# Attention heads: queries and keys in two F32R parts, scores as three passes over 64 rows

## The reference

```
q = einsum('bsd,hde->bhse', x, Wq)          # 16 heads, e = 64
k = einsum('bsd,hde->bhse', x, Wk)
v = einsum('bsd,hde->bhse', x, Wv)
scores = einsum('bhse,bhte->bhst', q, k) / sqrt(64), causal mask
out = softmax(scores) @ v
y = x + concat(out) @ Wo, then a layer norm with gamma and beta
```

## Time and profile before

| what | us |
|---|---|
| median of 3 runs | 995.03 (991.85 to 996.21) |
| the profiled execution, its own time | 994.27 |
| its span, first to last instruction | 992.5 |
| PE busy | 748.4 (75%) |
| DVE busy | 672.1 (68%) |
| ACT busy | 544.9 (55%) |
| POOL busy | 548.5 (55%) |
| PE waiting for xv_lo before value slices, 255 to 845 us | 14.9 (6 times) |
| DVE waiting for PE's masks before the maxima, 255 to 845 us | 162.8 (178 times) |
| ACT waiting for DVE's maxima, 255 to 845 us | 211.0 (180 times) |

### The profile page before, as it was taken

The page is one execution under the profiler, slowest core; times in us unless marked ns, Lnnn a source line. Parts: engine busy times, 40 slices in busy tenths (PEclk is TensorE's granted clock), DMA queues, the critical chain, the costliest instruction groups (busy, mean ns, idle before and its releaser), DMA issues.

```text
span 992.5 us, 21450 instructions
## 1 busy us (share of the span) xinstructions
PE 748.4 (75%) x7600; PEld 541.5 (55%) x7600; DVE 672.1 (68%) x1398; ACT 544.9 (55%) x1511; POOL 548.5 (55%) x552
## 2 busy tenths in 40 slices
PE   2567667427999998998999999999899996223232
PEld 2356555324576666775776766667676765122122
DVE  1579787844776776776677677677677875366755
ACT  0457566534665665665566566566566664054553
POOL 2166655621665565555555566555466665488862
PEclk9588878657999999999999999999999999555555
DMA  8111111011989999889789899798798998101101
GB/s 185 40 44 43 42 43 43 32 42 47 145 151 166 135 157 157 134 144 167 117 150 160 135 142 153 142 151 136 147 153 147 152 155 145 53 32 64 53 22 32
DMA packets 371461, 108.15 MB, mean 109 GB/s; under 512 B 348448, under 2 KB 365344, under 8 KB 371360
## 3 DMA queue, kind: packets, MB, share of 16 engines
q1 hardware_dynamic: 368096, 104.73, 58.8%
q10 hardware_dynamic: 3264, 2.10, 0.8%
HBM read 8.73 MB, written 2.10 MB: 11 GB/s over the span
## 4 chain that ended last, share of the span: by engine, by line
PE 45%; SPq 17%; POOL 11%; DVE 11%; issue 6%; DMA 5%; ACT 4%; POOLq 0%; DVEq 0%; ACTq 0%
PE wide L822 11%; SPq L998 7%; SPq L995 7%; PE bank L162 4%; PE bank L869 4%; PE bank L164 3%; PE bank L163 3%; PE wide L827 3%; PE bank L847 2%; PE bank L196 2%; POOL fn_y L355 2%; PE bank L849 2%; PE bank L848 2%; DMA prob_t<-prob_hl 2%; DVE ffn_g L422 2%
## 5 line engine op out<-in xcount | busy, mean ns | idle before, releaser
L975 POOL TENSOR_TENSOR prob_hl<-prob,prob_hl 128x768 f16<-128x768 f32 (+1 forms) x192 | 346.9, 1807 | 266.3 <-DVE prob_hl L927 266.3
L906 ACT ACTIVATE prob<-wide,neg_max 128x128 f32<-128x128 f32 (+3 forms) x512 | 264.0, 524 | 218.4 <-DVE neg_max L939 218.0
L939 DVE TENSOR_REDUCE neg_max<-wide 128x2 f32<-128x256 f32 (+3 forms) x256 | 205.4, 823 | 166.5 <-PE wide L827 166.3
L822 PE MATMUL wide<-k_sb,q_sb 64*128 64x128 f32 (+3 forms) x1024 | 193.4, 476 | 1.0 <-DVE k_sb L804 0.9
L847 PE MATMUL bank<-v_hi,prob_t 128*128 128x64 f16 x1280 | 134.9, 194 | 11.9 <-DMA prob_t<-prob_hl 11.4
L848 PE MATMUL bank<-v_lo,prob_t 128*128 128x64 f16 x1280 | 134.9, 194 | 0.0
L849 PE MATMUL bank<-v_hi,prob_t 128*128 128x64 f16 x1280 | 134.9, 194 | 0.0
L847 PEld LDWEIGHTS bank<-v_hi,prob_t 128*128 128x128 f16 x1280 | 117.5, 99 | 14.6 <-issue 12.5
L927 DVE CAST prob_hl<-prob 128x768 f16<-128x768 f32 (+1 forms) x192 | 119.6, 623 | 1.1 <-ACT prob L906 1.0
L849 PEld LDWEIGHTS bank<-v_hi,prob_t 128*128 128x128 f16 x1280 | 115.7, 99 | 0.0
L848 PEld LDWEIGHTS bank<-v_lo,prob_t 128*128 128x128 f16 x1280 | 115.6, 99 | 0.0
(11 more groups left out here) (184 smaller groups left out, 1468.4 us busy)
## 6 DMA issues: line engine op xcount, KB each, us to landing
prob_t<-prob_hl SPq DMA_TRANSPOSE x384, 3.2
x_next<-in_L_attn_a_in_features SPq DMA_DIRECT2D x8, 256.0 KB, 3.0
x_attn<-in_L_attn_a_in_features SPq DMA_DIRECT2D x8, 256.0 KB, 3.0
x_sb<-x_done SPq DMA_DIRECT2D x8, 256.0 KB, 2.3
y_res<-bn_y SPq DMA_DIRECT2D x8, 256.0 KB, 2.3
at_y<-y_res SPq DMA_DIRECT2D x8, 256.0 KB, 2.3
x_attn<-x_sb SPq DMA_DIRECT2D x8, 256.0 KB, 2.3
out_x<-x_done SPq DMA_DIRECT2D x8, 256.0 KB, 2.3
```

The source lines that it names most:

```text
L822: pe.matmul(dst[:, h, c:c + m], q[e, i * P:(i + 1) * P], k[e, 0:m], start=(i == UNIT_ROWS[u][0]), stop=False)
L906: last = act.activation(prob_2[s][:, at:at + m], score_banks(p, s)[:, h, c:c + m], ACT.Exp, bias=neg_max[p % 2][:, h, i:i + 1], accum_out= ...
L939: last = dve.tensor_reduce(neg_max[p % 2][:, :, i:i + 1], score_banks(p, s)[:, :, c:c + m], AX.X, ALU.max, negate=True)
L975: pool.tensor_tensor(prob_hl[u][:, w:2 * w], prob_2[u][:, 0:w], prob_hl[u][:, 0:w], ALU.subtract)\
```

## The change

- q_sb and k_sb are replaced by q_hi, q_lo, k_hi, k_lo (F32R, two buffers each). ACT writes q_hi from PSUM with the scale; DVE writes q_lo by a scalar_tensor_tensor, PSUM times the scale less q_hi, at the end of its s=0 work. ACT writes k_hi at s=1 behind the exponentials; DVE writes k_lo = PSUM less k_hi where it copied the keys.
- The K projection now waits for q_lo, the next Q projection and the scores for k_lo too.
- Each score matmul in fp32 becomes three in F32R, with the two heads alternating. The 128 keys of block 0 are widened to 256 (the second half is not read), so block 1 moves to column 256 of the bank.
- The copies xv_hi, xv_lo and their DMAs and wait are gone: value slices read xt_hi and xt_lo directly at the next batch's columns.
- x_beta of the back stage gets no memory of its own any more and lies in prob_2[2]. Branches for a loop variable that isn't an integer go.

```diff
-PAIR_AT = {0: 0, 1: 128, 2: 0, 3: 0}
+PAIR_AT = {0: 0, 1: 256, 2: 0, 3: 0}
...
         def values_tensor(pe, b, p):
             n = number(b, p)
-            wait(pe, "xv_in", 32 * (b + 1))
...
-            x = slice(p // 2 * P, (p // 2 + 1) * P)
+            x = slice((b + 1) * S + p // 2 * P, (b + 1) * S + (p // 2 + 1) * P)
...
-            split_product(pe, MB, xv_hi[:, x], xv_lo[:, x], wv_b_hi[:, half], wv_b_lo[:, half])\
+            split_product(pe, MB, xt_hi[:, x], xt_lo[:, x], wv_b_hi[:, half], wv_b_lo[:, half])\
...
         def project_tensor(pe, b, p, parts, done):
-            wait(pe, *(("k_sb", n) if done == "q_ps" else ("q_sb", n + 1)))
+            wait(pe, *(("k_lo", n) if done == "q_ps" else ("q_lo", n + 1)))
...
         def queries_scalar(act, b, p):
             wait(act, "q_ps", n + 1)
             wait(act, "s2", n - 1)
-            act.activation(q_sb[p % 2][:, :], QK, ACT.Copy, scale=float(E) ** -0.5).then_inc(sem("q_sb"), 1)
+            act.activation(q_hi[p % 2][:, :], QK, ACT.Copy, scale=float(E) ** -0.5).then_inc(sem("q_hi"), 1)
+
+        def queries_vector(dve, b, p):
+            n = number(b, p)
+            wait(dve, "q_hi", n + 1)
+            dve.scalar_tensor_tensor(out=q_lo[p % 2][:, :], in0=QK, scalar=float(E) ** -0.5,
+                                     in1=q_hi[p % 2][:, :].bitcast(F32), op0=ALU.mult, op1=ALU.subtract)\
+                .then_inc(sem("q_lo"), 1)
+
+        def keys_scalar(act, b, p):
+            n = number(b, p)
+            wait(act, "k_ps", n + 1)
+            wait(act, "s2", n - 1)
+            act.copy(k_hi[p % 2][:, :], QK).then_inc(sem("k_hi"), 1)
 
         def keys_vector(dve, b, p):
             n = number(b, p)
-            wait(dve, "k_ps", n + 1)
-            wait(dve, "s2", n - 1)
-            dve.tensor_copy(k_sb[p % 2][:, :], QK).then_inc(sem("k_sb"), 1)
+            wait(dve, "k_hi", n + 1)
+            dve.tensor_tensor(k_lo[p % 2][:, :], QK, k_hi[p % 2][:, :].bitcast(F32), ALU.subtract)\
+                .then_inc(sem("k_lo"), 1)
 
         def pair_scores(pe, b, p, u):
...
             for i in UNIT_ROWS[u]:
-                c, m = PAIR_AT[i], (i + 1) * P
-                for h in range(2):
-                    e = slice(h * E, (h + 1) * E)
-                    pe.matmul(dst[:, h, c:c + m], q[e, i * P:(i + 1) * P], k[e, 0:m], start=(i == UNIT_ROWS[u][0]),
-                              stop=False)
+                c, m = PAIR_AT[i], max(2, i + 1) * P
+                rows = slice(i * P, (i + 1) * P)
+                for a, (q, k) in enumerate(((qh, kh), (qh, kl), (ql, kh))):
+                    for h in range(2):
+                        e = slice(h * E, (h + 1) * E)
+                        pe.matmul(dst[:, h, c:c + m], q[e, rows], k[e, 0:m],
+                                  start=(i == UNIT_ROWS[u][0] and a == 0), stop=False)
...
         def heads_scalar(act, b, p):
                 if s == 0 and pair_exists(*later(b, p)):
                     queries_scalar(act, *later(b, p))
+                if s == 1 and pair_exists(*later(b, p)):
+                    keys_scalar(act, *later(b, p))
                 if s == 1 and pair_exists(*earlier(b, p, 2)):
                     wait(act, "ctx_t_ps", n - 1)
                     wait(act, "y_ps", n - 2)
                     act.copy(ctx_t[:, :], MB[:, :]).then_inc(sem("ctx_t"), 1)
...
         def heads_vector(dve, b, p):
                         values_vector(dve, bv + 1, pv, MB)
+                    if pair_exists(*later(b, p)):
+                        queries_vector(dve, *later(b, p))
                 if s == 1 and pair_exists(*later(b, p)):
                     keys_vector(dve, *later(b, p))
...
         def heads_sync(sp, b, p):
-            if p == 0 and (not isinstance(b, int) or b < B - 1):
-                wait(sp, "v_ps", VSLICES * (b + 1))
-                wait(sp, "bn_xt_lo", B)
-                for dst, src in ((xv_hi, xt_hi), (xv_lo, xt_lo)):
-                    sp.dma_start(dst[:, :].bitcast(F32), src[:, bass.ds((b + 1) * S, S)].bitcast(F32))\
-                        .then_inc(sem("xv_in"), 16)
...
-        x_beta = sb("x_beta", [P, QB, P])
+        x_beta = prob_2[2][:, 0:512].rearrange("p (a d) -> p a d", d=P)
```

More of the change, by code:

```diff
@@ L153, in hybrid_kernel @@
         prob_t = [sb(f"prob_t{u}", [P, 16, P], F16) for u in range(NU)]
[L154 to L157, removed]
+        q_hi = [sb(f"q_hi{k}", [P, S], F32R) for k in range(2)]
+        q_lo = [sb(f"q_lo{k}", [P, S], F32R) for k in range(2)]
+        k_hi = [sb(f"k_hi{k}", [P, S], F32R) for k in range(2)]
+        k_lo = [sb(f"k_lo{k}", [P, S], F32R) for k in range(2)]
         ctx_sb = sb("ctx_sb", [P, QB, 2, E])
@@ L728, in pair_exists @@
         def pair_exists(b, p):
-            return not isinstance(b, int) or 0 <= HP * b + p < PAIRS
+            return 0 <= HP * b + p < PAIRS
         def earlier(b, p, n):
@@ L767, in values_tensor @@
             n = number(b, p)
-            wait(pe, "xv_in", 32 * (b + 1))
-            if isinstance(b, int) and n < 2:
+            if n < 2:
                 wait(pe, "v_lo", n + VSLICES)
             wait(pe, "ctx_t", n - 1)
-            x = slice(p // 2 * P, (p // 2 + 1) * P)
+            x = slice((b + 1) * S + p // 2 * P, (b + 1) * S + (p // 2 + 1) * P)
             half = slice(p % 2 * 512, (p % 2 + 1) * 512)
-            split_product(pe, MB, xv_hi[:, x], xv_lo[:, x], wv_b_hi[:, half], wv_b_lo[:, half])\
+            split_product(pe, MB, xt_hi[:, x], xt_lo[:, x], wv_b_hi[:, half], wv_b_lo[:, half])\
                 .then_inc(sem("v_ps"), 1)
@@ L809, in pair_scores @@
             if u == 0:
-                wait(pe, "q_sb", n + 1)
-                wait(pe, "k_sb", n + 1)
+                wait(pe, "q_lo", n + 1)
+                wait(pe, "k_lo", n + 1)
             if u == 2:
@@ L816, in pair_scores @@
             dst = score_banks(p, u)
-            q, k = q_sb[p % 2], k_sb[p % 2]
+            qh, ql, kh, kl = q_hi[p % 2], q_lo[p % 2], k_hi[p % 2], k_lo[p % 2]
             for i in UNIT_ROWS[u]:
-                c, m = PAIR_AT[i], (i + 1) * P
-                for h in range(2):
-                    e = slice(h * E, (h + 1) * E)
-                    pe.matmul(dst[:, h, c:c + m], q[e, i * P:(i + 1) * P], k[e, 0:m], start=(i == UNIT_ROWS[u][0]),
-                              stop=False)
+                c, m = PAIR_AT[i], max(2, i + 1) * P
[5 more added lines that the diff above has]
+                                  start=(i == UNIT_ROWS[u][0] and a == 0), stop=False)
             for i in UNIT_ROWS[u]:
@@ L855, in context_turn_tensor @@
             wait(pe, "ctx", n + 1)
[L856 to L859, removed]
+            wait(pe, "v_lo", min(n + 2 + VSLICES, PAIRS))
             transposes(pe, MB, ctx_sb[:, :, :, :].rearrange("p a h e -> p (a h e)"), QB).then_inc(sem("ctx_t_ps"), 1)
@@ L890, in heads_tensor @@
                         context_turn_tensor(pe, *earlier(b, p, 2))
-                if s == 2 and (not isinstance(b, int) or b < B - 1):
+                if s == 2 and b < B - 1:
                     values_tensor(pe, b, p)
@@ L957, in heads_vector @@
                     bv, pv = before
-                    if not isinstance(bv, int) or 0 <= bv < B - 1:
+                    if 0 <= bv < B - 1:
                         values_vector(dve, bv + 1, pv, MB)
+                    if pair_exists(*later(b, p)):
+                        queries_vector(dve, *later(b, p))
                 if s == 1 and pair_exists(*later(b, p)):
                     keys_vector(dve, *later(b, p))
-                if s == 1 and p == 2 and (not isinstance(b, int) or b > 0):
+                if s == 1 and p == 2 and b > 0:
                     wait(dve, "y_ps", n - 2)
@@ L979, in heads_sync @@
             n = number(b, p)
-            if p == 0 and (not isinstance(b, int) or b < B - 1):
-                wait(sp, "v_ps", VSLICES * (b + 1))
-                wait(sp, "bn_xt_lo", B)
-                for dst, src in ((xv_hi, xt_hi), (xv_lo, xt_lo)):
-                    sp.dma_start(dst[:, :].bitcast(F32), src[:, bass.ds((b + 1) * S, S)].bitcast(F32))\
-                        .then_inc(sem("xv_in"), 16)
             if pair_exists(b, p):
-                if not isinstance(b, int):
-                    sp.to_reg(n)
-                    sp.to_reg(n + 1)
                 for u in range(NU):
@@ L1166, in _ @@
             queries_scalar(act, 0, 0)
+            keys_scalar(act, 0, 0)
             over_pairs(act, heads_scalar)
@@ L1177, in _ @@
                 values_vector(dve, 0, k, VB[k % len(VB)])
+            queries_vector(dve, 0, 0)
             keys_vector(dve, 0, 0)
```

## The result

The kernel after takes 1002.13 us (median of 4 runs, 1001.76 to 1003.28) against 994.68 us for the kernel before beside it: a ratio of 1.008, 95% interval 1.0056 to 1.0105. It is slower by 7 to 8 us. The forecast was 998, with slower as the likeliest of the three signs.

The account below looks back on a forecast made before the run. PE bound the old kernel at 8.93 us a pair; VectorE-ScalarE handovers would bind the new at 9.3. 56 x 9.3 + 7 x 8.9 + 4.2 = 587.3 against 585.3, plus 1.4 start-up: +3.4, 998 us, range 982 to 1014.

Parts of the forecast that it names:

- the three signs: Whole kernel: chances for the measured outcome, faster 0.18, same (990 to 1000 us) 0.36, slower 0.46.
- the round of 9.2 to 9.4: Heads stage: each pair of heads takes 9.2 to 9.4 us, giving 992 to 1004 us; chance 0.57.
- Where the change pays: Batch changes in the heads stage: removing xv copies and their wait gives back 25 us while PE sets the beat.
- Scores: PE's score matmuls: three split passes with heads side by side save 0.2 to 0.3 us, pair 8.93 to about 8.65.
- The rival of passes that don't overlap: PE's scores: the two heads' passes run one after another, pair 10.7 us, some 1090 us; chance 0.06.
- Now they hand over four times a pair: VectorE and ScalarE, in order, pass q and k parts to each other; this round sums to 9.29 us a pair.
- Does PE make a longer round? ... 9.10: Round over PE: 5.38 from scores to K projection plus 3.72 to next scores, 9.10 us, under 9.3.
- The last batch: Seven pairs without value slices: v_hi leaves the round, VectorE's own order is longer, 8.9 us a pair.
- I charge nothing for the clock: PE's new waits before the K projection, about 0.6 us a pair, were taken not to lower its clock.
- The start-up term: Once, before the first scores: q_lo delays the K projection 0.77 us and k_hi the keys 0.61, together 1.4.
- The cast that meets GpSimd: Rival: VectorE's unit 2 cast waits for GpSimd's subtraction, 0.1 to 0.4 us a pair; 9.5 gives 1009 us; chance 0.24.
- The range: Whole kernel: 982 to 1014 us, from 9.05 us a pair with q_lo at its lower bound to 9.55.

Follow-up runs that it names:

- the other round shortened: Kernel after, with context transposes moved before the K projection and ScalarE's ctx_t copy before the exponentials of s=1: 997.16 us, ratio 1.007, beat 9.25.
- both edits: Kernel after, with context transposes and ctx_t copy moved earlier and k_hi written by VectorE: 974.38 us (0.984), then 971.84 us (0.979) in a second run.

## Why the prediction came out right, and where it was off

998 us was forecast and 1002 measured, slower, which had the highest chance of the three signs (0.46), and the beat of 9.37 lies in the round of 9.2 to 9.4 that had the highest chance. Part of that is luck. The prediction found the right kind of cause, a closed round of handovers that is longer than PE's work, and dismissed the round that turned out to be the longest; with a wait that it had left out, that one is by chance only 0.08 us longer than the one it summed.

- **Where the change pays: right.** The xv copies gave back 23 us where 25 was said, with the beat of 8.93 unchanged.
- **Scores: right in size.** The heads' passes overlap, in either order. PE's pair went from 8.93 to 8.70; about 8.65 was said. The widened u=0 takes 0.91, inside the 0.86 to 0.98 given. The rival of passes that don't overlap is dead.
- **"Now they hand over four times a pair": right as a mechanism, wrong as the longest round.** The sum over VectorE and ScalarE was 9.29. With the other round shortened it measured 9.25; q_lo takes 0.69 us, not 0.74 (below), which is that difference. But in the kernel after the longest round goes over PE, and leaving k_lo out, which is only in VectorE's round, left the usual beat at 9.37.
- **"Does PE make a longer round? ... 9.10": the step that failed.** Read from the kernel after (PE's rows above, with the rows of DVE and ACT here), the round is q_lo to K projection 0.75, K projection to scores u=0 4.00, to max 1.34, to exponentials 1.06, to q_hi 1.60, to q_lo 0.64: 9.39. The first scores to the K projection are 5.39 where 5.38 was said; the K projection to the next scores is 4.00 instead of 3.72. Of these 0.28, 0.23 sit between the masks of u=2 and the value slice, 0.87 us where it was 0.64 (the earlier trace rows has the masks at 429.98; the slice came at 430.62):

```profile
428.33 0.58 ACT L810 CAST k_hi<-bank 128x512 fp32r<-128x512 f32 x1
428.80 0.60 ACT L929 COPY ctx_t<-bank 128x512 f32<-128x512 f32 x1
...
432.76 0.37 ACT L917 ACTIVATE prob<-wide,neg_max 128x128 f32<-128x128 f32 x1
...
434.36 0.61 ACT L797 ACTIVATE q_hi<-bank 128x512 fp32r<-128x512 f32 x1
```

```profile
425.61 0.69 DVE L802 SCALAR_TENSOR_TENSOR q_lo<-bank,q_hi 128x512 fp32r<-128x512 f32 x1
...
428.95 0.69 DVE L815 TENSOR_TENSOR k_lo<-bank,k_hi 128x512 fp32r<-128x512 f32 x1 [1.31 <-ACT k_hi L810]
...
431.70 1.02 DVE L952 TENSOR_REDUCE neg_max<-wide 128x2 f32<-128x256 f32 x2 [0.47 <-PE wide L841]
432.64 0.88 DVE L940 CAST prob_hl<-prob 128x1024 f16<-128x1024 f32 x1
...
435.00 0.69 DVE L802 SCALAR_TENSOR_TENSOR q_lo<-bank,q_hi 128x512 fp32r<-128x512 f32 x1 [0.22 <-ACT q_hi L797]
```

The value slice waits for the ctx_t copy, since both use one PSUM bank. That copy started at 429.41 in the old order and was done long before PE needed it; behind k_hi it runs from 428.80 to 429.40 against a slice that PE could have started at 429.23 (0.64 after the masks, as before), and does at 429.46. The prediction asked whether the ctx_t copy fits into ScalarE's time, found that it does, and did not ask who waits for it. It was worth 0.23 us of PE's time a pair, and lifted the round over PE from 9.14 (9.10 by the sum) past the other one, at 9.25, to 9.37. The kernel with k_hi on VectorE shows it: the wait is gone and the beat is 9.14. By these numbers the prediction's round would be the longest if the ctx_t copy alone were out of the way; that kernel wasn't run.
- **The last batch: right.** 8.83 was the usual beat, 8.9 was said (the mean of 8.97 has the y_res addition in it and other longer beats). The y_res addition costs 0.5 a batch, 0.6 was said.
- **"I charge nothing for the clock": wrong at the start.** The waits before the first K projection and the first scores, 0.69 and 0.88 us before the change, are 1.41 and 1.49, and the clock of 239 to 250 us is 0.53, where it was 1.00:

```profile
239.00:250.00 11.00, 9.17 (x62) 4.83 (x63) 6.96 (x12) 6.01 (x23) 3.30 (x2) 1.00 0.30 56
```

The first two beats, 9.87 and 10.19, are 1.3 us over the others together. (Before they were 7.53 and 8.17, since PE has less to do there; the sum took 9.3 for them.) The start-up term itself, 1.4, was right: from the first Q projection to the first scores it is 4.73 us where it was 3.39. In the steady state nothing had to be charged: the clock is 1.00 at 28.58 of 30 us.
- **The cast that meets GpSimd: it happens, and costs nothing.** The cast of unit 2 takes 0.88 here (0.95 in the mean of 400 to 800 us) against 0.68. GpSimd's subtraction of unit 1 runs 431.31 to 432.97, and the cast ends 0.55 after it. VectorE still idles 0.22 us before q_lo for ScalarE. The slack was there.
- **The range.** Its lower end, 9.05, isn't what its reason gives: q_lo at its lower bound makes the round 9.23. Nothing hangs on it.

The rows for these points, first the start (PE), then the cast and q_lo from 400 to 800 us:

```profile
237.46 0.50 PE L162 MATMUL bank<-xt_hi,wk_parts 128*128 128x512 f32 x1 [1.41 <-DVE q_lo L802]
...
239.92 0.58 PE L836 MATMUL wide<-k_hi,q_hi 64*128 64x256 f32 x2 [1.49 <-DVE k_lo L815]
```

```profile
L940 DVE CAST prob_hl<-prob 128x1024 f16<-128x1024 f32 x43 | 40.7, 948 | 0.9
...
L802 DVE SCALAR_TENSOR_TENSOR q_lo<-bank,q_hi 128x512 fp32r<-128x512 f32 x42 | 29.1, 692 | 8.3 <-ACT q_hi L797 7.8
```

The account: +0.075 us over 9.3 in 56 pairs is 4.2 us, +1.3 at the start, +0.5 in the last batch with its y_res addition, and -1.3 for the other six (2.9 us, where 4.2 was taken for all seven). That takes the first to last group from the forecast 587.3 to 592.0 (591.9 measured).

So a gain of 23 us at seven places was spent in 56 pairs, where PE, with 0.23 us less to do, waits 0.67 (9.37 - 8.70): 0.23 for ctx_t, and the other 0.44 for q_lo. What the xv copies would cost in the split kernel, whose PE has that slack, stays open: it wasn't tried.

## What to carry to other kernels

When an operand is split into parts, the copies out of PSUM turn into a relay between two engines, and every engine that runs in order passes the delay to what is queued behind it. Walk each closed round through all engines, and for every instruction that is moved or gets a new one ahead of it, ask who waits for its result, not only whether its engine has time for it. Then cut the handovers: writing both key parts on one engine was faster here than sharing them (9.14 against 9.37), at more work for the busier engine. Alone it gained by letting another copy start earlier; it took both edits to bring the beat down to PE's own work of 8.70.

Try each part of a change alone: the part that looked like tidying (reading xt where it lies) was the whole gain, 0.977 by itself. The split of queries and keys never came out ahead of that, even with its waits hidden (0.979 against 0.978).

## What the runs showed of the hardware

- Matmuls on rows 0 to 63 and on rows 64 to 127 run side by side even where the program has three of the one ahead of three of the other: 0.90 us for six passes of 512 columns, with starts in pairs (435.66, 436.00, 436.22). The Trainium skill, "TensorE: Matmul & The Clock Gate", Part 3, has matmuls start and end strictly in program order; this trace doesn't agree, if the compiled program has the order of the source.
- A scalar_tensor_tensor over 512 columns with a PSUM operand and an immediate scalar takes 0.692 us, the time of a tensor_tensor (k_lo: 0.692), not the 0.74 worked out from one with a scalar per partition (344 ns for 128 columns).
- Six DMA transposes a pair, all issued by SyncE, held the beat at 8.99 us in the mean at a DMA share of 0.93 to 0.95, though PE's work was 8.70; with five the mean was 8.84 at 0.78. SyncE's issues stood 1.34 us apart or more from 425 to 432 us, so that it, and not the DMA engines, may be what is short.
